# A fused attention and FFN block on one core: first load in halves, last matmul in two banks, new hand-written orders

## What is computed

```python
def _L0_attn_ref(x, ...):
    n  = _ln(x, ln_g, ln_b)
    W1 = _gelu(n @ h1_w1 + h1_b1) @ h1_w2 + h1_b2        # 128 -> 512 -> 128
    W2 = _gelu(n @ h2_w1 + h2_b1) @ h2_w2 + h2_b2
    W3 = jnp.tril(jnp.einsum('bzn,bsn->bzs', W1, W2))
    t  = _ln(_gelu(jnp.einsum('bzs,bsm->bzm', W3, n)), ln_g, ln_b)
    x1 = x + t
    return x + _mlp(_ln(x1, ln_g, ln_b), fm_w1, fm_b1, fm_w2, fm_b2)
def _L0_ffn_ref(x, ...):                                 # ternary weights, one scale per output
    h = silu(_tlin(x, w1_w, w1_s)) * _tlin(x, w2_w, w2_s)
    h = _gelu(_tlin(h, h1_w, h1_s))                      # 512 -> 512, "layer a"
    h = _gelu(_tlin(h, h2_w, h2_s))                      # 512 -> 512, "layer b"
    return _tlin(h, w3_w, w3_s)
x = x + _layernorm(_L0_attn_ref(_layernorm(x)))
x = x + _layernorm(_L0_ffn_ref(x))
```

## Time and profile before

| | |
|---|---|
| time, median of 3 runs | 378.2 us (377.82 to 378.77) |
| the profiled execution's own time | 379.27 us |
| its span (first to last instruction) | 377.5 us |
| PE busy | 363.0 us, 96% |
| DVE busy | 332.2 us, 88% |
| ACT busy | 298.0 us, 79% |
| POOL busy | 117.4 us, 31% |
| transfers | 9.27 MB, the first 50 us for nearly all of the loads |

### The profile page before, as it was taken

The page is one execution under the profiler, slowest core; times in us unless marked ns, Lnnn a source line. Parts: engine busy times, 40 slices in busy tenths (PEclk is TensorE's granted clock), DMA queues, the critical chain, the costliest instruction groups (busy, mean ns, idle before and its releaser), DMA issues.

```text
span 377.5 us, 5938 instructions
## 1 busy us (share of the span) xinstructions
PE 363.0 (96%) x1779; PEld 292.0 (77%) x1779; DVE 332.2 (88%) x977; ACT 298.0 (79%) x516; POOL 117.4 (31%) x186
## 2 busy tenths in 40 slices
PE   7999999989999999999999999999999999999991
PEld 7778787867887788877888778787877877777760
DVE  4999999999999987999999979797888899887643
ACT  3899698968679795998859689968898769777770
POOL 4530432532272017423531172006520362061111
PEclk9999999999999999999999999999999999999997
DMA  7572000000000001000000010000100000000001
GB/s 226 182 256 56 2 0 1 3 0 2 2 0 2 0 1 30 1 2 26 3 2 0 2 30 0 0 2 2 30 0 0 17 13 2 1 28 3 0 28 31
DMA packets 8529, 9.27 MB, mean 25 GB/s; under 512 B 560, under 2 KB 6320, under 8 KB 8496
## 3 DMA queue, kind: packets, MB, share of 16 engines
q1 hardware_dynamic: 8496, 8.87, 7.7%
HBM read 6.77 MB, written 2.10 MB: 23 GB/s over the span
## 4 chain that ended last, share of the span: by engine, by line
PE 76%; DVE 12%; ACT 4%; DMA 3%; issue 3%; POOL 1%; POOLq 0%; SPq 0%; DVEq 0%; ACTq 0%
PE bank L1124 10%; PE bank L1122 9%; PE bank L1137 8%; PE bank L1138 8%; PE bank L1024 5%; PE bank L1021 4%; PE bank L1022 4%; PE bank L954 4%; PE bank L1009 4%; PE bank L1005 4%; PE bank L1006 4%; PE bank L1105 4%; PE bank L1108 3%; PE bank L1048 3%; DMA raw<-ffn_w 2%
## 5 line engine op out<-in xcount | busy, mean ns | idle before, releaser
L431 ACT ACTIVATE h_hidden_hi<-bank,cols 128x512 fp32r<-128x512 f32 x64 | 43.3, 710 | 7.5 <-PE bank L1009 7.3
L627 DVE TENSOR_TENSOR ffn_gate_lo<-bank,ffn_gate_hi 128x512 fp32r<-128x512 f32 x64 | 42.5, 683 | 6.8 <-ACT bank L501 5.1
L627 DVE TENSOR_TENSOR h_hidden_lo<-bank,h_hidden_hi 128x512 fp32r<-128x512 f32 x64 | 42.0, 678 | 4.2 <-ACT bank L436 4.0
L436 ACT ACTIVATE bank<-bank,cols 128x512 f32<-128x512 f32 x64 | 42.5, 694 | 0.2
L501 ACT ACTIVATE bank<-bank,cols 128x512 f32<-128x512 f32 x64 | 42.0, 680 | 0.6
L1122 PE MATMUL bank<-ffn_gate_hi,ffn_w_hi 128*128 128x512 f32 x96 | 39.3, 409 | 0.8 <-ACT ffn_gate_hi L486 0.8
L1124 PE MATMUL bank<-ffn_gate_lo,ffn_w_hi 128*128 128x512 f32 x96 | 38.0, 396 | 1.0 <-DVE ffn_gate_lo L627 1.0
L495 ACT ACTIVATE ffn_h_hi<-bank,cols 128x512 fp32r<-128x512 f32 x32 | 21.6, 702 | 10.6 <-PE bank L1124 6.2
L301 POOL TENSOR_SCALAR ln_f_ve<-ln_f_mv 128x4 f32<-128x4 f32 x8 | 1.8, 228 | 85.4 <-DVE ln_f_mv L617 85.4
L627 DVE TENSOR_TENSOR ffn_h_lo<-bank,ffn_h_hi 128x512 fp32r<-128x512 f32 x32 | 21.3, 682 | 7.9 <-ACT bank L501 7.7
L1021 PE MATMUL bank<-h_hidden_hi,attn_w_lo 128*128 128x512 f32 x64 | 26.4, 412 | 1.2 <-DVE h_hidden_lo L627 1.2
(11 more groups left out here) (158 smaller groups left out, 1108.6 us busy)
## 6 DMA issues: line engine op xcount, KB each, us to landing
raw<-ffn_w SPq DMA_DIRECT2D x5, 512.0 KB, 3.6
out<-X SPq DMA_DIRECT2D x7, 256.0 KB, 2.3
raw<-attn_w SPq DMA_DIRECT2D x6, 256.0 KB, 5.4
X<-x SPq DMA_DIRECT2D x3, 256.0 KB, 5.2
raw<-ffn_w SPq DMA_DIRECT2D x1, 256.0 KB, 5.0
out<-X SPq DMA_DIRECT2D x2, 128.0 KB, 2.8
bc<-rows SPq DMA_DIRECT2D x1, 192.0 KB, 4.7
cols<-columns SPq DMA_DIRECT2D x1, 16.5 KB, 5.0
```

The source lines that it names most:

```text
L431: nc.scalar.activation(dst, bank(f"{L}u{j}", c)[:, :], ACT.Gelu, bias=bias_of(L, j)).then_inc(*hi[L].done(c, j))
L436: nc.scalar.activation(u[:, :], u[:, :], ACT.Gelu, bias=bias_of(L, j)).then_inc(*act2[L].done(c, j))
L627: return nc.vector.tensor_tensor(dst, whole, high.bitcast(f32), ALU.subtract)
```

## The change

1. **First x in halves.** SP loads tiles 0 and 1 of chunk 0, ACT's queue loads tiles 2 and 3 as ACT's first instruction; `x_st(0)` waits for the second half at tile 2.
2. **cols** are loaded after the first attention piece, not after the third.
3. **First transposes tile by tile.** `n_second` signals after each tile, `n_transpose` waits for each tile. Other waiters wait for the fourth tile. This holds for every chunk.
4. **Last w3 in two banks.** Columns 0:256 of the last w3 go to bank 6 and columns 256:512 to bank 5, so each of its 512-column matmuls is two of 256. ACT evicts the first half, DVE the second.
5. **Last store on two queues.** SP stores the first two tiles, ACT's queue the last two.
6. **Fills:** 35 to 26, 10 to 3, 11 to none, 9 to none.
7. **New tables** for the banks and for the order of work on POOL, ACT, DVE and PE, through all chunks. The work in them is the same.

```diff
-            x_piece(0, 0, 1)
+            sp.dma_start(X[:, 0:2, :], xv[:, 0:2, :]).then_inc(x_in[0], 16)
             sp.dma_start(bc[:, :, :], rows.rearrange(
...
             attn_piece(0)
+            sp.dma_start(cols[:, :], columns).then_inc(cols_in, 16)
             attn_piece(1)
             attn_piece(2)
-            sp.dma_start(cols[:, :], columns).then_inc(cols_in, 16)
...
-            for k in (0, 1):
-                half = slice(LAST * T + 2 * k, LAST * T + 2 * k + 2)
-                sp.wait_ge(*last_out.at(0, k))
-                sp.dma_start(ov[:, half, :], X[:, half, :]).then_inc(stored, 16)
+            sp.wait_ge(*last_out.at(0, 0))
+            sp.dma_start(ov[:, LAST * T:LAST * T + 2, :], X[:, LAST * T:LAST * T + 2, :]).then_inc(stored, 16)
...
         def _(act):
+            act.dma_start(X[:, 2:4, :], xv[:, 2:4, :]).then_inc(x_in_half, 16)
             act.wait_ge(*consts.at(0, 0))
...
-            def w3_evict_half(k):
+            def last_evict():
                 act.wait_ge(*fT.at(LAST - 1))
                 act.wait_ge(*w3.at(LAST))
-                half = slice(2 * k * P, 2 * (k + 1) * P)
-                nc.scalar.activation(OTF[:, half], bank("w3", LAST)[:, half], ACT.Copy, scale=cols[:, C_S3:C_S3 + 1]).then_inc(*last_evicted.done(0, k))
+                nc.scalar.activation(OTF[:, 0:2 * P], bank("w3", LAST)[:, 0:2 * P], ACT.Copy, scale=cols[:, C_S3:C_S3 + 1])\
+                    .then_inc(*evicted_a.done(0))
+            def last_store():
+                act.wait_ge(*last_out.at(0, 1))
+                act.dma_start(ov[:, LAST * T + 2:TILES, :], X[:, LAST * T + 2:TILES, :]).then_inc(stored, 16)
...
+            def last_evict_second():
+                dve.wait_ge(*fT.at(LAST - 1))
+                dve.wait_ge(*w3_second.at(0))
+                nc.vector.tensor_scalar(OTF[:, 2 * P:N], bank("w3b", LAST)[:, 2 * P:N], cols[:, C_S3:C_S3 + 1], None, ALU.mult)\
+                    .then_inc(*evicted_b.done(0))
...
-            fill("nT", 0, 35); n_transpose(0); fill("h1u0", 0, 10); up_mm("h1", 0, 0); ...
+            fill("nT", 0, 26); n_transpose(0); fill("h1u0", 0, 3); up_mm("h1", 0, 0); ...
```

More of the change, by code:

```diff
@@ L142, in bank @@
             return place[f"{group}.{c}"]
-        x_in = [sem(f"x_in{k}") for k in range(4)]
+        x_in, x_in_half = [sem(f"x_in{k}") for k in range(4)], sem("x_in_half")
         attn_in, ffn_in = [sem(f"attn_in{i}") for i in range(6)], [sem(f"ffn_in{i}") for i in range(FP)]
@@ L183, in sandwich_block @@
         o_shifted, f_rstd, x_out = steps("o_shifted", 2), steps("f_rstd", 4), steps("x_out")
-        last_evicted, last_shifted = steps("last_evicted", 2), steps("last_shifted")
+        w3_second, evicted_a, evicted_b, last_shifted = (steps(s) for s in ("w3_second", "evicted_a", "evicted_b", "last_shifted"))
         last_centred, last_out = steps("last_centred"), steps("last_out", 2)
@@ L670, in x_st @@
                 dve.wait_ge(*x_ready(c))
-                stats(x_stats, tile_of(xc(c)), LN["x"]["st"], c)
+                for t in range(T):
+                    if c == 0 and t == 2:
+                        dve.wait_ge(x_in_half, 16)
+                    last = nc.vector.bn_stats(LN["x"]["st"][:, t, :], X[:, c * T + t, :])
+                last.then_inc(*x_stats.done(c, 0))
             def x_ag(c):
@@ new lines, in _ @@
+            n_second(1); fm_bias_add(); ffn_w_lo(0); up_lo("h1", 2, 0); x_st(2); ffn_w_lo(1); x_ag(2); up_lo("h1", 3, 0)
+            up_lo("h2", 0, 0); up_lo("h2", 1, 0); up_lo("h2", 2, 0); down_lo("h1", 0); up_lo("h2", 3, 0); ffn_w_lo(2)
+            down_lo("h2", 0); nT_low(1); ffn_w_lo(3); score_mask(0, 0); score_mask(1, 0); ffn_w_lo(4); score_lo(0, 0)
+            score_lo(1, 0); ffn_w_lo(5); up_lo("h1", 0, 1); lo_test(); up_lo("h1", 1, 1); x_st(3); t_st(0); up_lo("h1", 2, 1)
+            t_ag(0); x_ag(3); n_first(2); up_lo("h1", 3, 1); n_second(2); up_lo("h2", 0, 1); lo_raise(); up_lo("h2", 1, 1)
@@ new lines, in _ @@
+            layer_lo("b", 0, 0); layer_lo("b", 1, 0); m_norm(2); up_lo("h1", 0, 4); y_ag(1); up_lo("h1", 1, 4)
+            up_lo("h1", 2, 4); mT_low(2); y_norm(1); layer_lo("b", 2, 0); n_first(5); up_lo("fm", 0, 2); yT_low(1)
+            up_lo("h1", 3, 4); layer_lo("b", 3, 0); up_lo("fm", 1, 2); gate_1(0, 1); gate_1(1, 1); x_st(7); gate_2(0, 1)
+            up_lo("fm", 2, 2); gate_2(1, 1); gate_lo(0, 1); gate_1(2, 1); gate_lo(1, 1); gate_1(3, 1); gate_2(2, 1)
+            gate_2(3, 1); gate_lo(2, 1); gate_lo(3, 1); n_second(5); down_lo("h1", 4); up_lo("h2", 0, 4); t_gain(3)
@@ L957, in n_transpose @@
             def n_transpose(c):
-                pe.wait_ge(*n_v_ready.at(c))
-                transposes(nT, "nT", lambda t: NF[:, t, :], c)
+                bank_free("nT", c)
+                for t in range(T):
+                    pe.wait_ge(*n_v_ready.at(c, t))
+                    last = nc.tensor.transpose(bank("nT", c)[:, t * P:(t + 1) * P], NF[:, t, :], ident[:, :])
+                last.then_inc(*nT.done(c))
             def m_transpose(c):
@@ L1126, in product, with last_product, term @@
                         last.then_inc(*(w3.done(c) if L == "w3" else layer[L].done(c, j)))
+                def last_product(k):
+                    if k == 0:
+                        bank_free("w3", LAST)
+                        bank_free("w3b", LAST)
+                    w = slice(F_W3 + k * P, F_W3 + (k + 1) * P)
+                    def term(weights, src, start=False, stop=False):
+                        for g, half in (("w3", slice(0, 2 * P)), ("w3b", slice(2 * P, N))):
+                            last = nc.tensor.matmul(bank(g, LAST)[:, half], weights[:, w], src[:, k, half], start=start, stop=stop)
+                            if stop:
+                                last.then_inc(*(w3.done(LAST) if g == "w3" else w3_second.done(0)))
+                    pe.wait_ge(*hi["b"].at(LAST, k))
+                    if lo_pass:
+                        term(Fw[1], HG[0], start=k == 0)
+                    term(Fw[0], HG[0], start=k == 0 and not lo_pass)
+                    pe.wait_ge(*lo["b"].at(LAST, k))
+                    term(Fw[0], HG[1], stop=k == J - 1)
                 def layer_mm(L, j, c):
@@ L1230, in stream @@
[L1230 to L1234 removed]
+                up_mm("h1", 0, 2); up_mm("h1", 1, 2); scores(0, 1); scores(1, 1); up_mm("h1", 2, 2); up_mm("h1", 3, 2)
```

519 lines of the change are left out of this document (255 added, 264 removed), and 43 rows, old and new, of the table TURNS.

## The result

The changed kernel took 376.49 us (median of 20 runs, 375.74 to 379.59), the kernel before 378.75 beside it (20 runs, 377.37 to 379.36). The ratio is 0.9959, 95% interval 0.9944 to 0.9973: faster by 0.41%, or 1.55 us of 378.2. The forecast was 377.2, a change of −1.0. The two medians lie 2.26 us apart, the means (377.01 and 378.57) 1.56. The ratio goes with the means, and they are pulled by a group of slower runs of the changed kernel, which the experiments take up.

The account below looks back on a forecast made before the run. DVE was taken to bound 10 to 98 us, PE 98 to 343 us. Terms −0.3 + 0.2 + 0 − 0.35 − 0.55 = −1.0 us against the median of 378.2 gave 377.2 us, 8-in-10 range 374.6 to 380.6.

Parts of the forecast that it names:

- the order term: Up to 98 us: new order changes only DVE's idle time, +1.0 at 27 us, −0.8 from better fits, together +0.2 us.
- What bounds the kernel: Whole kernel: DVE bounds 10 to 98 us with 2.05 us idle; PE bounds 98 to 343 us.
- The start: Before 10 us: halved x load lets `bc` be issued and land earlier, −0.3 us; earlier `cols` and tile-wise transposes gain nothing.
- The fills: Up to 98 us: 36 fills dropped, those not at the start hide behind DVE, 0; without that cover 1.8 us.
- The walk at 27 us: Chunk 1's aT_hi behind both FFN weight pieces: aT_lo done at 29.6, PE stands about 2 us, DVE idles 1.0 us more.
- The rival in which the prefix shortens: Up to 98 us: gate_half ahead of n_tok_lo (1.1 us) and 1.0 us of DVE idle closed, 375.5 us; chance 0.17.
- the gate's stall: At the start on DVE: gate_half stands still until POOL's n_tok_lo ends, costing 1.1 us; forecast kept it, rival removed it.
- The clock: At the start: fewer fills delay PE's rise to 2.4 GHz, 24 up products take twice 0.23 us, 380.7 us; chance 0.10.
- The last w3: After 368 us: two banks, ACT and DVE evicting at the same time, bring the statistics sooner, −0.35 us.
- The last store: At the end: second store no longer loses time behind the first on SP (issue 1.43 us), −0.55 us.

Follow-up runs that it names:

- the changed kernel again: The changed kernel, unedited, measured once more beside its own variants on the same chip: 376.6 us, ratio 0.9957 to the kernel before.

## Why the prediction was right, and where it was not

The direction, the size (−1.0 against −1.55) and the bound held. That the size came out near is in part luck: the order term had the wrong sign and is off by 1.5 us, and the loss by the clock, which the sum put at nothing, took some of that back. Nor do the terms add as the sum takes for granted. Measured singly in the kernel before, the parts give +1.5 us (the tables), −0.3 (start and two banks), −0.2 (store) and +0.2 (fills), +1.2 together; all of them at once give −1.55. The order needs the new start to gain at all, and the old fills take part of its gain away.

**What bounds the kernel:** right. With the clock up, 258 DVE instructions took 84.68 of 85.85 us, and the middle stayed full.

**The start:** −0.3 forecast. The pair of profiles gives −0.63, the mean over fourteen profiles −0.45. The size is right, but not the reason first given: `bc` was not issued earlier, it was issued at 1.27 us in all fourteen, and only landed sooner, at 4.6 to 5.5 us instead of 5.2 to 6.0. gate_half behaved as said, 1.26 us and ended with n_tok_lo. That the earlier `cols` and the tile-wise transposes bring nothing there is what the trace shows.

**The fills:** "so they hide behind DVE: 0" was right for the kernel before (1.0006) and wrong for the new order, where nine of them cost 0.76 us. The clock, which falls in some runs without them, was not in the term either. Their price was taken from the old order; it depends on what the new one puts beside them.

**The order up to 98 us:** +0.2 forecast, −1.34 measured with the clock up (order and dropped fills together). This is the step that failed. The walk at 27 us has the sequence right and the times wrong. The rows of ACT, DVE and PE in the changed kernel again, with the clock up:

```profile
24.17 1.69 ACT L401 ACTIVATE ffn_w_hi<-raw 128x1024 fp32r<-128x1024 f32 x2
26.43 0.59 ACT L413 ACTIVATE aT_hi<-bank 128x512 fp32r<-128x512 f32 x1
```

```profile
27.23 0.68 DVE L635 TENSOR_TENSOR aT_lo<-bank,aT_hi 128x512 fp32r<-128x512 f32 x1
29.07 0.43 DVE L729 TENSOR_TENSOR bank<-bank,mask 128x256 f32<-128x256 f32 x1 [0.21 <-PE bank L1056]
```

```profile
26.66 0.62 PE L1081 MATMUL bank<-ffn_w_lo,ones_r 128*1 128x256 f32 x4 [0.85 <-DVE lo_max L655]
28.87 0.45 PE L1026 MATMUL bank<-aT_hi,attn_w_lo 128*128 128x512 f32 x1
```

The piece landed at 24.10 us, not at 25.5, so ACT began 1.3 us sooner than in the walk, and aT_lo started at 27.23 instead of ending at 29.6. PE stood for 1.0 us (0.85 and 0.18), not 2, and chunk 1's products began at 28.87, where the walk leads to some 30.4. (In the first profile they began at 30.79, but only because the clock had made it late; that this is near the walk is chance.) What the walk puts as "runs out too, and I count 1.0 us more idle time of DVE" was 0.2 us of waits there. In sum DVE's idle time fell by 0.85 us, and its work took 0.49 us less. Which of the better fits brought that was not found. The rival in which the prefix shortens (375.5) was half right: its 1.0 us of closed idle time was 0.85, while the gate's stall, its other half, stayed.

**The clock:** given 0.10 as a case of its own for the whole kernel. It is a state of single executions: up to 12 of 32 runs of the changed kernel. In the profiled one it cost 1.84 us (forecast of the rival +3.5, for 24 slow products; seven were slow). The rival's sign, first products 0.45 us apart, was seen (0.43), but not its mechanism. It had the rise come late for want of fills; the first two products were 0.31 us apart, as before, and the clock fell after them, in PE's wait for aT_lo. The falls are why the gain is 0.41% and not the 0.6% that the terms with the clock up would give: 0.45 + 1.34 + 0.21 + 0.4 = 2.4 us. The runs agree: those of the changed kernel with a mean clock of 0.992 or more have medians 2.4 and 2.0 us below that of the kernel before, in the two sets.

**The last w3:** −0.35 forecast, −0.21 measured twice. DVE's 256-column eviction took 0.48 us and ended at 369.04, after ACT's at 368.90, so the second half is ready 0.14 us behind the first and not with it.

**The last store:** −0.55 forecast, −0.4 by the means, −1.0 in the pair of profiles. The rule of the Trainium skill, "DMA: Bandwidth & Descriptors", section "Issuing engines are not separate DMA queues", read strictly (next to nothing) cannot be told from this by the runs. The profiles speak for 0.4, and what is saved is the sequencer's time, as that section says, only that it was not small here: 0.92 to 1.43 us on SP against 0.4 on ACT's queue.
